# A two-pass attention and MLP kernel on one core: A's block turn moved to the end of the next slot, and u with all that follows one slot later

## The chip, the cores and the metric

The kernel runs on one core of one Trainium2 chip. Its time is the device time of one execution in microseconds; the number to predict is the median of the runs.

## The reference

There are 64 batches, each with x and ctx of 128 x 512 (float32). Every batch goes through the same two layers:

```python
# layer 0, one batch: x_c = x, x_s = ctx (C = 128 rows, T = 512 columns)
Mn = Wn @ inorm(x_c) + bn;  Mm = Wm @ inorm(x_s) + bm
A  = softmax(Mn.T @ Mm, axis=-1)              # 512 x 512
Mo = (Wl @ x_s + bl) @ A.T
x  = Wo @ Mo + bo + x_c
# layer 1: x attends to ctx with 16 heads of 32, then an MLP 512 -> 2048 -> 512
q = LN1(x) @ q_w + q_b;  k = ctx @ k_w + k_b;  v = ctx @ v_w + v_b
hidden = softmax(q k.T / sqrt(32), masked) v @ cproj_w + cproj_b + x
out = hidden + gelu(LN2(hidden) @ fc_w + fc_b) @ proj_w + proj_b
```

## The kernel before

Two passes follow each other. `attention_pass` computes `hidden` for all batches and stores it; `mlp_pass` reads it back in 16 groups of four batches. The change touches only the first pass.

The first pass is a software pipeline written out by hand. Slot `s` handles several batches at once: `b0` is batch s, `b1` batch s-1, up to `b5`, batch s-5 (six in flight); `ahead` is batch s+1. Every engine has its own `slot(s)` with a fixed order of instructions, and engines meet only at semaphores. The slots -1 to 5 are written out, then come loop turns of four slots, then the last ones up to `LAST` = B + 4 = 68. The sum of what one slot does in steady state, in TensorE's order:

- the scores S1 of b4 (mask matmuls and `qT` x `kT`, L1055 and L1060), V of b2, the turn of the normalised x1 of b2 (L999), the two small projections M of b0, one half of the key or query projection of a pair of batches (`qk(0)`; keys in even slots, queries in odd ones), the scores S0 of b0, the product of probabilities and V of b5 (L1101), u = ctx x A.T of b1 (twelve matmuls of 512 columns from `at_hi`, `at_lo`, `ctxT_hi`, `ctxT_lo`), `qk(1)`, layer 0's output (`out0`, which needs `u_hi` and `u_lo`) of b1, and the output projection (`cproj`) of b5.

Each large matmul is made of three passes over an upper and a lower half of each operand (fp32r); the upper half is made by ScalarE, the lower one by VectorE (DVE) or GpSimd (POOL).

A, the softmax of b0, has to be turned (transposed) before it can be used. ScalarE writes the exponentials (L728) and scales them (L747) into `A`; SP writes `A` to `a_turn` in memory in two halves (`write_a`, L497) and reads it back in blocks into `a_blocks` in the next slot (`read_a`, L504, which first waits until that batch's data is in memory and until `at_lo` of the batch before has been computed). DVE then turns 32 x 32 blocks in place (`turn_a`, L844, four instructions), ScalarE makes `at_hi` (`upper_at`, L712), POOL `at_lo` (`lower_at`, L599). The probabilities of layer 1 take the same way through `p_turn` and `p_blocks` (`turn_probs`, L820). All transfers are issued by SP, in the order of its `slot`. DVE's slot has `turn_a(0)` and `turn_a(1)` right behind the lower half of M (L869), `turn_probs` after them, then `turn_a(2)`, `turn_a(3)`, and only then the four `maximum0` (L837) on which the softmax of b0 waits. `ctx` is turned at the end of b0's own slot (L928).

## Time and profile before

| | |
|---|---|
| median of 3 runs | 3541.45 us (3538.01 to 3541.54) |
| the profiled execution | 3546.0 us, span of its instructions 3543.8 us |
| first pass, about | 0 to 2133 us |
| second pass, about | 2133 to 3544 us |
| TensorE busy | 3001.6 us (85%) |
| DVE busy | 1894.7 us (53%) |
| ScalarE busy | 1494.3 us (42%) |
| POOL busy | 1102.1 us (31%) |

The busy times are sums over both passes. TensorE's clock has two levels; the column PEclk gives the share of the higher one that was granted.

### The profile page before, as it was taken

How to read it: one execution, taken by the hardware profiler on the slowest of the kernel's cores; microseconds unless marked ns; L12 is line 12 of the kernel's file. 1: busy time of each engine (PE TensorE's matmuls, PEld its weight loads, DVE VectorE, ACT ScalarE, POOL GpSimd, SP SyncE). 2: the span in 40 equal slices, each digit the busy share in tenths (PEclk: the TensorE clock that was granted, in tenths of full speed). 3: DMA queues.
4: the chain of work that ended last, by engine and by line, in shares of the span. 5: the costliest groups of instructions: out<-in, count | busy, mean ns of one | idle time of the engine just before them, and what ended most of it. 6: DMA issues, size and time to landing. Idle time of an engine off the chain costs nothing. (4 is left out here: it accounts for less than half of the span.)

```text
span 3543.8 us, 54659 instructions
## 1 busy us (share of the span) xinstructions
PE 3001.6 (85%) x17527; PEld 2458.7 (69%) x17527; DVE 1894.7 (53%) x3705; ACT 1494.3 (42%) x4210; POOL 1102.1 (31%) x998
## 2 busy tenths in 40 slices
PE   6777787778777777787778759999999999999999
PEld 4666666656566666666666647888888888888887
DVE  5666666666666666666666645333333333333332
ACT  4665556556655665566556633111111111111111
POOL 4554445444444544444444422000000000000000
PEclk8988898898889888998989878999999999999999
DMA  6555665566566655666566552111111111111110
GB/s 174 162 165 163 176 179 163 163 175 176 160 167 181 173 165 165 181 177 164 168 178 179 161 159 94 39 38 37 36 36 36 36 36 36 36 36 36 36 41 18
DMA packets 440819, 416.04 MB, mean 117 GB/s; under 512 B 155200, under 2 KB 319552, under 8 KB 440768
## 3 DMA queue, kind: packets, MB, share of 16 engines
q1 hardware_dynamic: 440768, 415.40, 42.5%
q8 instruction: 27, 0.44, 0.1%
q14 instruction: 24, 0.20, 0.0%
HBM read 231.79 MB, written 167.77 MB: 113 GB/s over the span
## 5 line engine op out<-in xcount | busy, mean ns | idle before, releaser
L1308 ACT ACTIVATE gl<-pre,fc_bias 128x512 f32<-128x512 f32 x256 | 176.6, 690 | 1119.2 <-PE pre L1393 1119.2
L1347 DVE CAST hT_hi<-gl 128x512 fp32r<-128x512 f32 x256 | 109.3, 427 | 839.8 <-ACT gl L1308 839.8
L599 POOL TENSOR_TENSOR at_lo<-a_blocks,at_hi 128x512 fp32r<-128x512 f32 x256 | 323.0, 1273 | 507.2 <-ACT at_hi L712 499.9
L1101 PE MATMUL bank<-y,stage 128*32 128x128 f32 x2048 | 123.0, 419 | 405.3 <-DVE y L820 405.3
L675 ACT ACTIVATE rows<-bank,negmax 128x128 f32<-128x128 f32 x1024 | 359.2, 365 | 125.1 <-DVE negmax L831 125.1
L1101 PEld LDWEIGHTS bank<-y,stage 128*32 128x32 f32 x2048 | 88.8, 167 | 436.7 <-DVE y L820 375.5
L844 DVE STREAM_TRANSPOSE a_blocks<-a_blocks 128x512 f32<-128x512 f32 x256 | 164.0, 680 | 391.1 <-DMA a_blocks<-a_turn 391.1
L712 ACT ACTIVATE at_hi<-a_blocks 128x512 fp32r<-128x512 f32 x256 | 156.3, 630 | 445.4 <-DVE a_blocks L844 445.4
L590 POOL TENSOR_TENSOR rows<-rows,rsum 128x512 f32<-128x512 f32 x256 | 263.5, 1039 | 225.0 <-DVE rsum L827 225.0
L1392 PE MATMUL pre<-yT_hi,rest_lo 128*128 128x512 f32 x768 | 299.0, 389 | 0.0
L1391 PE MATMUL acc<-rest_lo,hT_hi 128*128 128x512 f32 x768 | 298.9, 389 | 0.0
L1393 PE MATMUL pre<-yT_hi,rest_hi 128*128 128x512 f32 x768 | 298.9, 389 | 0.0
L1393 PE MATMUL acc<-rest_hi,hT_hi 128*128 128x512 f32 x768 | 298.9, 389 | 0.0
L1391 PE MATMUL pre<-yT_lo,rest_hi 128*128 128x512 f32 x768 | 298.9, 389 | 0.0
L1392 PE MATMUL acc<-rest_hi,hT_lo 128*128 128x512 f32 x768 | 298.8, 389 | 0.0
L177 POOL TENSOR_TENSOR rstd<-ve,neghalf 128x4 f32<-128x4 f32 x16 | 16.3, 1018 | 870.9 <-DVE ve L171 870.9
L618 POOL TENSOR_TENSOR normed_lo<-x_ctx,normed_hi 128x512 fp32r<-128x512 f32 x128 | 164.1, 1302 | 309.6 <-ACT normed_hi L752 309.6
L747 ACT ACTIVATE rows<-rows,rsum 128x512 f32<-128x512 f32 x256 | 164.1, 712 | 120.7 <-DVE rsum L920 120.7
L675 ACT ACTIVATION_READ_ACCUMULATOR rows<-bank,negmax 128x1 f32 x1024 | 210.9, 206 | 0.0
L831 DVE TENSOR_REDUCE negmax<-bank 128x4 f32<-128x512 f32 x256 | 169.1, 683 | 44.9 <-PE bank L1060 44.9
L1268 POOL TENSOR_TENSOR rows<-rows,proj_bias 128x512 f32<-128x512 f32 x64 | 83.0, 1299 | 326.2 <-DVE y L183 321.2
L1349 DVE TENSOR_TENSOR hT_lo<-gl,hT_hi 128x512 fp32r<-128x512 f32 x256 | 177.3, 693 | 8.8
(158 smaller groups left out, 8189.2 us busy)
## 6 DMA issues: line engine op xcount, KB each, us to landing
a_turn<-rows SPq DMA_DIRECT2D x128, 512.0 KB, 7.6
a_blocks<-a_turn SPq DMA_DIRECT2D x256, 256.0 KB, 5.1
p_turn<-rows SPq DMA_DIRECT2D x128, 512.0 KB, 3.0
p_blocks<-p_turn SPq DMA_DIRECT2D x256, 256.0 KB, 5.9
x_ctx<-in_x SPq DMA_DIRECT2D x64, 256.0 KB, 2.6
x_ctx<-in_ctx SPq DMA_DIRECT2D x64, 256.0 KB, 2.8
blocks<-in_ctx SPq DMA_DIRECT2D x256, 64.0 KB, 5.7
small<-in_x SPq DMA_DIRECT2D x64, 256.0 KB, 6.0
```

Of the source, the lines that this page charges most:

```text
L590: pool.tensor_tensor(probs[:, :, r, :, :], probs[:, :, r, :, :], rsum1[:, r, :].unsqueeze(1).unsqueeze(3).to_broadcast([P, 4, 4, 32]), ALU ...
L599: pool.tensor_tensor(by_rows(at_lo, j), a_chunks[:, j], by_rows(at_hi, j).bitcast(F32), ALU.subtract).then_inc(at_lo_set, 1)
L618: pool.tensor_tensor(normed_lo[:, i, :], normed[:, i, :], normed_hi[:, i, :].bitcast(F32), ALU.subtract).then_inc(normed_lo_set, 1)
L675: act.activation(probs[:, :, r, c, :], by_chunk(S1_BANK[r])[:, c, :].rearrange("p (d b) -> p d b", b=32), ACT.Exp, bias=negmax1[:, r, c:c ...
L747: act.activation(A[:, :, t, :], A[:, :, t, :], ACT.Identity, scale=rsum0[:, t:t + 1]).then_inc(a_scaled, 1)
L831: dve.tensor_reduce(negmax1[:, r, :], by_chunk(S1_BANK[r]), AX_X, ALU.max, negate=True).then_inc(max1_set, 1)
L1101: mm = pe.matmul(bank[PV_BANK][32 * r:32 * r + 32, c * P:(c + 1) * P], v_sb[:, b5.quarter, h * HD:(h + 1) * HD], pT[:, r, c, :], start=Tru ...
L1308: act.activation(gl[:, i % 2, :], pre[i % 2][:], ACT.Gelu_apprx_tanh, bias=mlp.fc_bias[:, i:i + 1]).then_inc(gelu_done, 1)
L1349: dve.tensor_tensor(hT_lo[:, i % 2, :], gl[:, i % 2, :], hT_hi[:, i % 2, :].bitcast(F32), ALU.subtract).then_inc(hT_lo_set, 1)
L1391: pe.matmul(out, a_hi, b_lo, start=first, stop=False)
L1392: pe.matmul(out, a_lo, b_hi, start=False, stop=False)
L1393: return pe.matmul(out, a_hi, b_hi, start=False, stop=last)
```

## The change

`LOOPED` and `LAST` go from 6 and B + 4 to 7 and B + 5, so the pass has 71 slots instead of 70, and seven batches are in flight. The names are shifted: `a1` is batch s-1, and `b1` to `b5` now mean s-2 to s-6. What belongs to A's turn (`turn_a`, `upper_at`, `lower_at`) and to ctx's turn works on `a1`; u, out0, x1, V, queries, keys, S1 and all behind it work on the shifted names and so come one slot later for a given batch. `turn_a` moves in DVE's slot from before `turn_probs` and `maximum0` to behind `rsum0` and around the normalisation of `ahead`; `upper_at` and `lower_at` move to the end of ScalarE's and POOL's slots. `read_a` stays where it is, at the start of the next slot. TensorE's order of operations is unchanged. No instruction is added to a batch and none is taken away.

```diff
-        FIRST, LOOPED, LAST = -1, 6, B + 4
+        FIRST, LOOPED, LAST = -1, 7, B + 5
@@ sync, slot(s): read_a(s-1) stays first
-                e = s + -1          # x_res
+                e = s + -2
-                e = s + -3          # mask
+                e = s + -4
-                if (s + -4).exists():
-                    write_probs(s + -4, 0)
-                    write_probs(s + -4, 1)
+                if (s + -5).exists():
+                    write_probs(s + -5, 0)
+                    write_probs(s + -5, 1)
...
-                e = s + 1
+                e = s
                 if e.exists() and e.has_before(1):
                     load_blocks(e)
-                e = s + -5          # hidden
+                e = s + -6
@@ gpsimd, slot(s)
-                normalise(0)
-                lower_at(0)
-                normalise(1)
-                lower_at(1)
-                lower_at(2)
-                lower_at(3)
-                normalise(2)
-                normalise(3)
+                for r in range(4):
+                    normalise(r)
                 (in_rstd of ahead)
+                lower_at(0)
+                lower_at(1)
                 (normed_lo of ahead, x1_rstd, x1b, ctxT_lo of a1)
+                lower_at(2)
+                lower_at(3)
@@ scalar, slot(s)
                 exp1(1)
-                upper_at(0)
-                upper_at(1)
                 exp1(2)
                 qk_bias(0)
-                upper_at(2)
-                upper_at(3)
                 exp1(3)
                 exp0(0)
                 exp0(1)
+                exp0(2)
+                exp0(3)
                 (outT_hi of b5)
-                exp0(2)
-                exp0(3)
-                (u_hi of b1)
                 (the four scalings of A)
+                (u_hi of b1)
+                upper_at(0)
+                upper_at(1)
+                qk_bias(1)
+                upper_at(2)
+                upper_at(3)
                 (normed_hi of ahead)
-                qk_bias(1)
                 (ctxT_hi of a1, was b0)
@@ vector, slot(s)
-                turn_a(0)
-                turn_a(1)
                 sum1_reciprocal(1)
                 turn_probs(0..3)
-                turn_a(2)
-                turn_a(3)
-                sum1_reciprocal(2)
                 maximum0(0)
                 maximum0(1)
-                sum1_reciprocal(3)
+                sum1_reciprocal(2)
                 maximum0(2)
                 maximum0(3)
+                sum1_reciprocal(3)
                 (statistics of ahead)
+                (rsum0 of b0)
+                turn_a(0)
+                turn_a(1)
+                (outT_lo of b5)
                 (normed of ahead)
-                (outT_lo of b5)
-                (rsum0 of b0)
+                turn_a(2)
+                turn_a(3)
                 (u_lo of b1)
                 (ctx's turn, x1, mask, x1's statistics, hid: as before)
```

The lines in brackets stand for blocks of the kernel that are moved whole or stay. The first statements of the other engines' slots only change in which parity of s they act.

## Rows read from the trace of the kernel before

**Rows 1.** Stretches of the span: busy (instructions) of PE, PEld, DVE, ACT, POOL; PEclk; DMA share.
```profile
1000.00:1400.00 400.00, 306.73 (x2218) 249.68 (x2217) 264.62 (x524) 241.23 (x745) 190.28 (x174) 0.89 0.62 173
1022.00:1024.00 2.00, 0.00 (x0) 0.00 (x0) 2.00 (x4) 2.00 (x10) 2.00 (x2) 0.50 0.00 0
2300.00:3543.00 1243.00, 1238.60 (x5465) 1025.82 (x5463) 444.45 (x852) 199.15 (x283) 79.79 (x65) 1.00 0.14 35
```
**Rows 2.** The waits, 600 to 1800 us: total us, times, longest.
```profile
PE bank L1101 <- DVE y L820: 236.5, 38, 8.0
DVE a_blocks L844 <- DMA a_blocks<-a_turn: 232.2, 37, 7.8
```
**Rows 3.** DVE's timeline over one slot: start, us, operation, count, [idle before].
```profile
1020.40 1.30 DVE L844 STREAM_TRANSPOSE a_blocks<-a_blocks 128x512 f32<-128x512 f32 x2 [6.99 <-DMA a_blocks<-a_turn]
...
1021.69 2.46 DVE L820 STREAM_TRANSPOSE y<-p_blocks 128x512 f32<-128x512 f32 x4
...
1027.41 0.18 DVE L827 RECIPROCAL rsum<-sum 128x4 f32<-128x4 f32 x1 [0.85 <-ACT rows L675]
...
1031.42 1.00 DVE L909 TENSOR_SCALAR x_ctx<-x_ctx,in_mv,in_rstd 128x512 f32<-128x512 f32 x2 [0.82 <-POOL in_rstd L614]
1032.34 0.68 DVE L807 TENSOR_TENSOR m_lo<-bank,m_hi 128x512 fp32r<-128x512 f32 x1
...
1033.03 0.66 DVE L807 TENSOR_TENSOR m_lo<-bank,m_hi 128x512 fp32r<-128x512 f32 x1
...
1038.92 1.29 DVE L831 TENSOR_REDUCE negmax<-bank 128x4 f32<-128x512 f32 x2 [0.69 <-PE bank L1060]
1040.73 1.43 DVE L853 TENSOR_SCALAR x<-x,x_mv,x_rstd 128x512 f32<-128x512 f32 x1 [0.52 <-POOL stage L630]
...
1044.90 1.38 DVE L869 SCALAR_TENSOR_TENSOR m_lo<-bank,bias,m_hi 128x512 fp32r<-128x512 f32 x2
1053.09 1.30 DVE L844 STREAM_TRANSPOSE a_blocks<-a_blocks 128x512 f32<-128x512 f32 x2 [6.81 <-DMA a_blocks<-a_turn]
```
**Rows 4.** SP's timeline in the same slot: start and us of issuing the transfers.
```profile
1035.97 1.24 SPq L497 DMA_DIRECT2D a_turn<-rows  x2
...
1045.59 1.75 SPq L504 DMA_DIRECT2D a_blocks<-a_turn  x4
```
**Rows 5.** TensorE's timeline in the same slot.
```profile
1024.20 1.93 PE L1101 MATMUL bank<-y,stage 128*32 128x128 f32 x32 [7.13 <-DVE y L820]
...
1033.83 0.47 PE L968 MATMUL bank<-m_lo,small_hi 128*128 128x512 f32 x1 [1.04 <-DVE m_lo L807]
...
1037.57 0.40 PE L1055 MATMUL bank<-mask_less,masked_bf 1*128 1x512 bf16 x4
```
**Rows 6.** GpSimd's timeline in the same slot.
```profile
1036.31 2.56 POOL L618 TENSOR_TENSOR normed_lo<-x_ctx,normed_hi 128x512 fp32r<-128x512 f32 x2 [4.92 <-ACT normed_hi L752]
```
**Rows 7.** ScalarE's timeline in the same slot.
```profile
1033.14 2.56 ACT L747 ACTIVATE rows<-rows,rsum 128x512 f32<-128x512 f32 x4 [2.11 <-DVE rsum L920]
1035.62 1.13 ACT L752 ACTIVATE normed_hi<-x_ctx 128x512 fp32r<-128x512 f32 x2
```
**Rows 8.** The page's groups by cost: A's lower and upper halves, mean ns of one.
```profile
L599 POOL TENSOR_TENSOR at_lo<-a_blocks,at_hi 128x512 fp32r<-128x512 f32 x256 | 323.0, 1273 | 507.2 <-ACT at_hi L712 499.9
...
L712 ACT ACTIVATE at_hi<-a_blocks 128x512 fp32r<-128x512 f32 x256 | 156.3, 630 | 445.4 <-DVE a_blocks L844 445.4
```
**Rows 9.** DVE's timeline at the hid of slots 5, 63, 64 and 68.
```profile
162.36 0.69 DVE L954 TENSOR_TENSOR hid<-bank,stage 128x512 f32<-128x512 f32 x1 [0.74 <-PE bank L970]
...
2032.03 0.69 DVE L954 TENSOR_TENSOR hid<-bank,stage 128x512 f32<-128x512 f32 x1 [0.72 <-PE bank L970]
...
2063.13 0.69 DVE L954 TENSOR_TENSOR hid<-bank,stage 128x512 f32<-128x512 f32 x1 [0.71 <-PE bank L970]
...
2132.91 0.68 DVE L954 TENSOR_TENSOR hid<-bank,stage 128x512 f32<-128x512 f32 x1
```
**Rows 10.** The waits, 0 to 145 us.
```profile
DVE a_blocks L844 <- DMA a_blocks<-a_turn: 10.2, 3, 6.9
```

More of the change, by code:

```diff
@@ L533, in slot @@
                     load(e)
-                if (s + -4).exists():
-                    read_probs(s + -4)
+                if (s + -5).exists():
+                    read_probs(s + -5)
                 if s.exists():
@@ L564, in load_second_for_mlp @@
                 sp.dma_start(mlp_raw[1], mlp_stage_source(w, 1)).then_inc(mlp.staged[1], 16)
-            slots(sp, slot, {B + 1: load_for_mlp, B + 3: load_second_for_mlp})
+            slots(sp, slot, {B + 1: load_for_mlp, B + 4: load_second_for_mlp})
         @block.gpsimd
@@ L584, in slot @@
             def slot(s):
-                b0, b1, b2, b3, b4, ahead = s, s + -1, s + -2, s + -3, s + -4, s + 1
+                b0, a1, b1, b3, b4, ahead = s, s + -1, s + -2, s + -4, s + -5, s + 1
                 def normalise(r):
@@ L666, in slot @@
             def slot(s):
-                b0, b1, b2, b3, b4, b5, ahead = s, s + -1, s + -2, s + -3, s + -4, s + -5, s + 1
+                b0, a1, b1, b2, b3, b4, b5, ahead = s, s + -1, s + -2, s + -3, s + -4, s + -5, s + -6, s + 1
                 def exp1(r):
@@ L680, in qk_bias @@
                 def qk_bias(half):
-                    if s.parity == 0 and b1.exists() and b2.exists():
+                    if s.parity == 1 and b1.exists() and b2.exists():
                         act.wait_ge(k_done, b2.pair_nth(2, half + 1))
@@ L901, in slot @@
                     dve.tensor_scalar(in_ve[:], in_mv[:, :, 1], EPS, None, ALU.add).then_inc(in_veps, 1)
+                if b0.exists():
+                    dve.wait_ge(exp0_done, b0.nth(4, 4))
+                    if a1.exists():
+                        dve.wait_ge(a_scaled, a1.nth(4, 4))
+                    dve.reciprocal(rsum0[:], sum0[:]).then_inc(rsum0_set, 1)
+                turn_a(0)
+                turn_a(1)
+                if b5.exists():
+                    dve.wait_ge(outT_hi_set, b5.nth(1, 1))
+                    lower(outT_lo, bank[PV_BANK][:], outT_hi, outT_lo_set)
                 if ahead.exists():
@@ L910, in slot @@
                                           in_rstd[:, i:i + 1], ALU.subtract, ALU.mult).then_inc(normed_set, 1)
-                if b5.exists():
-                    dve.wait_ge(outT_hi_set, b5.nth(1, 1))
-                    lower(outT_lo, bank[PV_BANK][:], outT_hi, outT_lo_set)
-                if b5.exists() and not b4.exists():
-                    first_group()
-                if b0.exists():
-                    dve.wait_ge(exp0_done, b0.nth(4, 4))
-                    if b1.exists():
-                        dve.wait_ge(a_scaled, b1.nth(4, 4))
-                    dve.reciprocal(rsum0[:], sum0[:]).then_inc(rsum0_set, 1)
+                turn_a(2)
+                turn_a(3)
                 if b1.exists():
@@ L923, in slot @@
                     lower(u_lo, bank[U_BANK][:], u_hi, u_lo_set)
-                if b0.exists():
-                    dve.wait_ge(blocks_in, b0.nth(64, 64))
+                if b5.exists() and not b4.exists():
+                    first_group()
+                if a1.exists():
+                    dve.wait_ge(blocks_in, a1.nth(64, 64))
                     if b1.exists():
@@ L960, in statistics @@
                     mlp.lower_half(dve, mlp.first_lo[:, 0, c, :], mlp.first_hi[:, 0, c, :], 0, c, mlp_raw[0])
-            slots(dve, slot, {0: prepare_small, 2: prepare_q, LAST - 2: statistics})
+            slots(dve, slot, {0: prepare_small, 3: prepare_q, LAST - 2: statistics})
         @block.tensor
```

56 lines of the change are left out of this document (28 added, 28 removed).

## The prediction, made before the changed kernel ran

> **What bounds the kernel now.** I read the stretches first. In the second pass TensorE works all the time at the full clock; in the first pass every engine has gaps (TensorE 307 of 400 us, DVE 265, POOL 190) [rows 1]. So the second pass stays as it is, and the question is what paces a slot of the first. From slot 5 to slot 63 the hid of one batch follows the last after (2032.03 - 162.36) / 58 = 32.24 us [rows 9].
>
> The waits name two large ones of equal size: TensorE stands 236.5 / 38 = 6.2 us a slot until DVE has turned the probabilities, and DVE stands 232.2 / 37 = 6.3 us a slot for the blocks of A to come back from memory [rows 2]. They are one wait: DVE's order puts turn_a ahead of turn_probs and maximum0, so what waits for either waits for A's round trip [rows 3].
>
> The timelines close the circle. A's blocks of one slot are turned from 1020.40, those of the next from 1053.09: 32.69 us [rows 3]. In between: 15.57 us from the turn over maximum0, exp0, rsum0 and the scaling to the issue of the write at 1035.97, then 9.62 us until the write has landed and the read is issued at 1045.59, then 7.50 us until it has landed [rows 4]. The sum is 32.69, with no slack anywhere. This loop of work and two landings is the bound; TensorE's 7.13 us before L1101 [rows 5] are its consequence.
>
> **The change part by part.**
>
> *turn_a behind rsum0.* The round trip no longer stands before maximum0 of the same slot. DVE's wait of 6.99 us goes, if the blocks have landed by the new place. I time a new slot from its mask matmul (0; 1037.57 before). DVE reaches the end of L869 at 8.7, as before (1046.28) [rows 3]. Everything between 1020.40 and u_lo at 1033.03 is the same set of DVE operations in a new order, 12.63 us, of which two waits should go: 0.85 for ScalarE (the exponentials are no longer interleaved with upper_at) and 0.82 for in_rstd (two turns and outT_lo now stand in between) [rows 3]. That leaves 10.96. turn_a(0) comes behind this set without its four turns, outT_lo and the normalisation (about 4.0 us): at 8.7 + 7.0 = 15.7.
>
> *Loop 1, work.* maxima1 to the end of L869: 7.36 (1038.92 to 1046.28); the set: 10.96; start of u_lo to out0: 0.80 (1033.03 to 1033.83); out0 and cproj to the next mask matmul: 3.74; from there to maxima1: 1.35 [rows 3, 5]. Sum 24.21 us a slot. This is DVE nearly without a pause, closed by TensorE.
>
> *Loop 2, landings.* turn_a(0) to the end of the normalisation of ahead: two turns 1.29, outT_lo and a reciprocal 0.69, two normalisations 0.92 = 2.9; then load, read_probs and the issue of write_a, which SP holds in this order behind the normalisation: 3.63 (1032.34 to 1035.97); the two landings 9.62 and 7.50 [rows 3, 4]. Sum 23.65. At 24.2 a slot the blocks have landed 0.6 us before turn_a(0) wants them.
>
> *Loop 3, POOL.* lower_at(0) and (1) now stand ahead of normed_lo, and upper_at ahead of normed_hi. From x1n (1040.73) to the end of L869 5.55, to rsum0 7.0, four scalings 2.5, u_hi with four upper_at and qk_bias 3.5 (0.6 each, 0.8), normed_hi to POOL 0.7, and 4.42 from normed_lo to the next x1n (1036.31 to 1040.73) [rows 3, 6 to 8]. Sum 23.7. POOL's own two lower_at, 2.5 us, run beside ScalarE's part.
>
> *lower_at(2), (3) at POOL's end.* read_a of the next slot waits for them, and x_res, mask and write_probs are queued behind it on SP. POOL ends ctxT_lo about 4 us into the next slot and these at 6.5; the write of A lands at about 7.4 (issue at 22 of a 24.2 us slot, plus 9.62), so they cost nothing while they are under that; uncovered they would cost their excess.
>
> *TensorE.* 32.71 - 7.13 - 1.04 = 24.5 us without its two waits [rows 5], less what half clock costs L1101 and u now: after its pause the granted clock is 0.50 [rows 1]. With no pause over 1.1 us left I expect it to stay at 2.4 GHz, which takes TensorE to about 23 us. If the clock stayed low there, TensorE would be at 24.5 and set the same slot as loop 1, so either answer is inside the range.
>
> *The DVE and POOL overlap.* x1n takes 1.43 us where two of the same form take 1.00, the ones beside no POOL work [rows 3]. It overlaps POOL's work now and will again, so it stays at 1.43. The Trainium skill (SBUF — State Buffer, Who interferes with whom) says that such a DVE instruction and GpSimd hold a common port in turn, and the later one fully blocks. It speaks against the change, which moves more POOL work to that place: by it mask and normalisation could lose up to 0.9 us each. The normalisation falls where POOL has nothing yet; mask lies beside the cproj wait.
>
> *The slot.* Three loops and TensorE lie within 1.2 us of each other, 24.2 the longest. A tie of four is seldom met exactly, so I take 24.8 (0.6 is my allowance, an estimate; the ends are 24.0, all waits at their best, and 27.4, below).
>
> *Fill and drain.* There are 71 slots for 70, one more to fill and one more to drain. Fill: the first hid moves from slot 5 to slot 6, 162.36 + 32.24; against that slots 5 and 6 take 24.8 instead of 32.24, 2 x 7.4, and of the 10.2 us waited for A's blocks before 145 us [rows 10] I count 8 as gone. First hid at about 171.8. Then 57 slots of 24.8 to slot 63: 1413.6, at 1585.4. Slot 64 (no b0; before 31.1 [rows 9]) I put at 24 and slot 65 at 21, both estimates from loop 1 without maximum0 and M; the last four stay 2132.91 - 2063.13 = 69.8 [rows 9]. Last hid at 1700.2 instead of 2132.91: 432.7 us saved.
>
> The profiled execution took 3546.0 us, 4.5 more than the median of 3541.45. 3546.0 - 432.7 = 3113.3, and 4.5 less gives 3109 for the median. One microsecond of the slot is worth some 58 us.
>
> **The rivals.**
>
> *A. The landings grow (loop 2 sets).* For: the same bytes in fewer microseconds bring the DMA share from 0.62 [rows 1] to 0.62 x 32.24 / 24.8 = 0.81, and loop 2 is only 0.6 us below loop 1. Against: what is issued ahead of each of the two transfers, and in which order, stays the same, and between 1022 and 1024 the DMA engines do nothing [rows 1]. It decides once the two landings take over 0.6 us more. At 20% more (3.4 us on 17.1) the slot is 27.1 and the time 3109 + 2.3 x 58 = 3242; at 30%, in the proportion of the share, 28.8 and 3341. The Trainium skill (DMA: Bandwidth & Descriptors, Latency and other measured facts) gives memory access 0.2 us on average and 2 us at high load; by it two landings could rise by 3.6 us, 27.3 a slot and some 3250.
>
> *B. Better than the sum.* Slots at 23.0 to 23.9 us, if x1n and xnT_lo no longer wait (0.52 and more in loop 1) and all halves finish in time: 3109 - 1.3 x 58 = 3034 for 23.5.
>
> *C. The change doesn't take A off the path.* The blocks come later than turn_a(0) by much, since read_a waits for lower_at(3), now POOL's last. The wait then only moves down DVE's slot, in front of normed, u_lo and all that follows. Half of the gain stays: 28.5 to 30, some 3350.
>
> *D. Slower than before.* The same place, the landings on SP's one queue behind POOL's tail. Loop 2 has 17.12 us of landings; it becomes slower than before only when it passes about 32.7 us (the 0.5 above 32.24 for one more drain slot), so when the landings reach 26.2, 1.5 times theirs. At 34 us the time is 3546 + 1.8 x 58 - 4.5 = 3646. Against it: no transfer is added, and the DMA engines have slack.
>
> **How the numbers follow.** Forecast (slots 24.0 to 26.0, 3060 to 3180): 0.62. A: 0.24. B: 0.07. C: 0.04. D: 0.02, and 0.01 for no difference. The predicted time is 3109. The range runs from 3060 to 3255: it leaves out B and D, C and the upper part of A, together 0.2. Faster by over 0.2% (what a measurement of this kernel can tell from no change): 0.97; within it 0.01; slower 0.02.
>
> **What the profile would show.** Right: no wait for a_turn before L844, a slot of some 25 us between two hid, TensorE's wait before L1101 gone and the clock near 1.00 throughout the first pass, L1101 and the twelve matmuls of u at full speed; the largest wait left is TensorE's for u_lo, about 1 us. A would show as a wait of DVE before L844 in its new place, with landings longer than 9.6 and 7.5; C as the same wait of 4 us and more, with read_a issued only after lower_at(3); loop 3 as DVE waiting over 1 us for x1b before L853. The prediction is wrong in its mechanism if the slot stays above 30, and in a size if fill and drain cost more than the 45 us counted for slots 64 and 65.

## The result, and the profile after

| | before | after |
|---|---|---|
| median | 3539.73 us | 3037.14 us |
| runs | 3535.79 to 3541.54 | 3035.83 to 3039.05 |
| span of the profiled execution | 3543.8 us | 3034.5 us |

(The median before is that of the three runs given above and a fourth, 3535.79 us.) The ratio is 0.8582, with a 95% interval of 0.8567 to 0.8597: 502.6 us less. The forecast was 3109 us, the range 3060 to 3255. The direction and the place of the gain came out as forecast; the time is 72 us below the forecast and 23 below the range.

First the stretches of the changed kernel, in the columns of [rows 1] (busy time of PE, PEld, DVE, ACT and POOL, granted clock, DMA share, GB/s). The second pass still does what it did; the first pass has hardly a gap left on TensorE (378.52 of 400 us instead of 306.73), the clock is 1.00 instead of 0.89, and the DMA share has risen from 0.62 to 0.84.

```profile
1000.00:1400.00 400.00, 378.52 (x3004) 314.02 (x3003) 363.19 (x711) 321.01 (x1019) 264.37 (x238) 1.00 0.84 233
1600.00:3034.00 1434.00, 1414.00 (x6239) 1168.42 (x6228) 528.84 (x995) 242.28 (x351) 105.90 (x86) 0.99 0.15 40
```

The waits of the changed kernel between 600 and 1500 us, 38 slots (us in total, times, longest), answer [rows 2]. DVE's wait for A's blocks is 1.4 us in all where it was 6.3 us a slot; TensorE's wait for the turned probabilities is gone; TensorE's largest is now that for u_lo (m_lo, L805, is the helper's name for it), 1.2 us a slot.

```profile
POOL at_lo L599 <- ACT at_hi L710: 112.6, 38, 3.0
...
PE bank L966 <- DVE m_lo L805: 46.9, 38, 1.8
...
DVE x L931 <- PE bank L968: 22.4, 38, 1.0
DVE negmax L829 <- PE bank L1058: 20.9, 38, 0.6
...
DVE a_blocks L842 <- DMA a_blocks<-a_turn: 1.4, 3, 0.6
```

DVE's timeline over one ordinary slot answers [rows 3]: start, us, operation, [idle before and what ended it]. From maxima1 to maxima1 it is 1089.28 - 1065.63 = 23.65 us, and no pause in it is over 0.6 us. (Line numbers are those of the changed kernel, two below the old ones at this place: L829 is maxima1, the row maxima of the scores S1; L842 turn_a; L851 x1n, the normalisation of layer 0's output x1; L867 m_lo; L805 outT_lo, xnT_lo and u_lo. x1n has to wait for x1b, GpSimd's sum of x1 and cproj's bias, which is the tile `stage` at L626.)

```profile
1065.63 1.29 DVE L829 TENSOR_REDUCE negmax<-bank 128x4 f32<-128x512 f32 x2 [0.57 <-PE bank L1058]
1066.87 1.42 DVE L851 TENSOR_SCALAR x<-x,x_mv,x_rstd 128x512 f32<-128x512 f32 x1
...
1071.03 1.38 DVE L867 SCALAR_TENSOR_TENSOR m_lo<-bank,bias,m_hi 128x512 fp32r<-128x512 f32 x2
...
1079.61 1.30 DVE L842 STREAM_TRANSPOSE a_blocks<-a_blocks 128x512 f32<-128x512 f32 x2
...
1082.32 1.29 DVE L842 STREAM_TRANSPOSE a_blocks<-a_blocks 128x512 f32<-128x512 f32 x2
1083.54 0.65 DVE L805 TENSOR_TENSOR m_lo<-bank,m_hi 128x512 fp32r<-128x512 f32 x1
...
1086.79 0.65 DVE L939 TENSOR_SCALAR mask_less<-mask_u 128x128 bf16<-128x128 uint8 x1
...
1089.28 1.29 DVE L829 TENSOR_REDUCE negmax<-bank 128x4 f32<-128x512 f32 x2 [0.57 <-PE bank L1058]
```

TensorE's rows of the same slot answer [rows 5]. The 32 matmuls on the probabilities take 1.08 us instead of 1.93 and start without a wait.

```profile
1076.00 1.08 PE L1099 MATMUL bank<-y,stage 128*32 128x128 f32 x32
1084.33 0.47 PE L966 MATMUL bank<-m_lo,small_hi 128*128 128x512 f32 x1 [1.44 <-DVE m_lo L805]
1087.92 0.40 PE L1053 MATMUL bank<-mask_less,masked_bf 1*128 1x512 bf16 x4
```

SP's rows answer [rows 4]: the write of A is issued at 1062.15, the read at 1071.19, and the turn starts at 1079.61, so from issue to turn there are 17.46 us for the two landings, and nothing else of their slot stands behind them. In the median of 30 slots (batches 20 to 49) the last block has landed 0.7 us before the turn starts. Behind SP's rows stand GpSimd's rows of the piece that matters below (it answers the place of [rows 6]): x1b is done at 1066.77, 0.10 us before x1n starts, and the last lower halves of A end at 1070.70, 6.4 us into the slot, where the prediction had 6.5.

```profile
1062.15 1.22 SPq L497 DMA_DIRECT2D a_turn<-rows  x2
...
1071.19 1.74 SPq L504 DMA_DIRECT2D a_blocks<-a_turn  x4
```
```profile
1065.46 1.31 POOL L626 TENSOR_TENSOR stage<-x,cproj_bias 128x512 f32<-128x512 f32 x1
1066.71 1.30 POOL L629 TENSOR_TENSOR ctxT_lo<-small_t,ctxT_hi 128x512 fp32r<-128x512 f32 x1
1067.96 2.74 POOL L599 TENSOR_TENSOR at_lo<-a_blocks,at_hi 128x512 fp32r<-128x512 f32 x2
```

The hids of slots 6, 63, 64 and 69 of the changed kernel answer [rows 9]. A mean slot is (1511.96 - 163.64) / 57 = 23.65 us; the median of the 57 is 23.57.

```profile
163.64 0.69 DVE L952 TENSOR_TENSOR hid<-bank,stage 128x512 f32<-128x512 f32 x1 [0.20 <-PE bank L968]
...
1511.96 0.69 DVE L952 TENSOR_TENSOR hid<-bank,stage 128x512 f32<-128x512 f32 x1 [0.73 <-PE bank L968]
...
1533.58 0.69 DVE L952 TENSOR_TENSOR hid<-bank,stage 128x512 f32<-128x512 f32 x1 [0.71 <-PE bank L968]
...
1623.57 0.68 DVE L952 TENSOR_TENSOR hid<-bank,stage 128x512 f32<-128x512 f32 x1
```

Last, the page's DMA rows, first of the kernel before and then of the changed one (KB each, median us from issue to landing). With 35% more bytes a microsecond A's two landings are what they were; only the write of the probabilities became longer, 3.0 to 4.5 us.

```profile
a_turn<-rows SPq DMA_DIRECT2D x128, 512.0 KB, 7.6
a_blocks<-a_turn SPq DMA_DIRECT2D x256, 256.0 KB, 5.1
p_turn<-rows SPq DMA_DIRECT2D x128, 512.0 KB, 3.0
```
```profile
a_turn<-rows SPq DMA_DIRECT2D x128, 512.0 KB, 7.6
a_blocks<-a_turn SPq DMA_DIRECT2D x256, 256.0 KB, 5.0
p_turn<-rows SPq DMA_DIRECT2D x128, 512.0 KB, 4.5
```

### The profile page after: what moved, and what is told of

It is laid out like the page before. It is cut to its first block and busy times, and to the rows that moved or that the text cites. A ratio compares the mean times of both kernels' runs of the same rounds, so it can differ in the third digit from the quotient of the medians.

```text
span 3034.5 us, 54536 instructions
## 1 busy us (share of the span) xinstructions
PE 2864.3 (94%) x17527; PEld 2369.3 (78%) x17527; DVE 1910.4 (63%) x3705; ACT 1469.5 (48%) x4210; POOL 1119.3 (37%) x998
## 5 line engine op out<-in xcount | busy, mean ns | idle before, releaser
L599 POOL TENSOR_TENSOR at_lo<-a_blocks,at_hi 128x512 fp32r<-128x512 f32 x256 | 335.4, 1330 | 190.1 <-ACT at_hi L710 190.1
L673 ACT ACTIVATION_READ_ACCUMULATOR rows<-bank,negmax 128x1 f32 x1024 | 239.9, 234 | 0.0
L829 DVE TENSOR_REDUCE negmax<-bank 128x4 f32<-128x512 f32 x256 | 169.0, 682 | 36.7 <-PE bank L1058 36.7
L722 ACT ACTIVATE rows<-bank,negmax 128x512 f32<-128x512 f32 x256 | 178.0, 782 | 10.5 <-DVE negmax L835 10.5
L842 DVE STREAM_TRANSPOSE a_blocks<-a_blocks 128x512 f32<-128x512 f32 x256 | 166.2, 687 | 8.3 <-DMA a_blocks<-a_turn 7.6
L614 POOL TENSOR_TENSOR normed_lo<-x_ctx,normed_hi 128x512 fp32r<-128x512 f32 x128 | 162.2, 1289 | 23.5 <-ACT normed_hi L751 23.4
L835 DVE TENSOR_REDUCE negmax<-bank 128x1 f32<-128x512 f32 x256 | 161.4, 667 | 10.2 <-PE bank L968 10.1
L1389 PEld LDWEIGHTS pre<-yT_lo,rest_hi 128*128 128x128 f32 x768 | 144.3, 188 | 30.0
```

The lines of the kernel that those rows point to most:

```text
L599: pool.tensor_tensor(by_rows(at_lo, j), a_chunks[:, j], by_rows(at_hi, j).bitcast(F32), ALU.subtract).then_inc(at_lo_set, 1)
L673: act.activation(probs[:, :, r, c, :], by_chunk(S1_BANK[r])[:, c, :].rearrange("p (d b) -> p d b", b=32), ACT.Exp, bias=negmax1[:, r, c:c ...
L722: act.activation(A[:, :, t, :], by_chunk(S0_BANK[t]), ACT.Exp, bias=negmax0[:, t:t + 1], accum_out=sum0[:, t:t + 1]).then_inc(exp0_done, 1)
L829: dve.tensor_reduce(negmax1[:, r, :], by_chunk(S1_BANK[r]), AX_X, ALU.max, negate=True).then_inc(max1_set, 1)
L842: dve.transpose(a_chunks[:, j], a_chunks[:, j]).then_inc(at_turned, 1)
L1389: pe.matmul(out, a_hi, b_lo, start=first, stop=False)
```

## The experiments

All ratios are to the kernel before on the same chip. The interval of each is about 0.15% to either side, some 5 us, so two kernels within 8 us of each other aren't told apart by their times; the slots of their traces (one execution each) then help a little further. The two half changes have one run each and no interval. The mean slot is taken over the 57 slots up to slot 63 (58 in the kernels with the old pipeline), the median over the same.

| kernel | median us | ratio, 95% interval | mean slot | median slot |
|---|---|---|---|---|
| before | 3539.73 | | 32.24 | 32.31 |
| changed | 3037.14 | 0.8582, 0.8567 to 0.8597 | 23.65 | 23.57 |
| turns early again | 3546.28, one run | | 31.78 | 31.73 |
| orders alone | 3471.09, one run | | 30.71 | 30.72 |
| A's write first on SP | 3032.31 | 0.8565, 0.8551 to 0.8579 | 23.60 | 23.58 |
| normed halves first | 3029.16 | 0.8546, 0.8531 to 0.8562 | 23.54 | 23.52 |
| u_lo first | 3046.10 | 0.8603, 0.8587 to 0.8618 | 23.79 | 23.59 |
| u_lo and mask first | 3046.61 | 0.8599, 0.8583 to 0.8615 | 23.84 | 23.58 |
| x1n alone | 3031.42 | 0.8565, 0.8547 to 0.8583 | 23.52 | 23.54 |
| one more DVE instruction | 3091.45 | 0.8722, 0.8705 to 0.8739 | 24.57 | 24.08 |
| the same, eight batches a turn | 3108.87 | 0.8774, 0.8751 to 0.8797 | 24.94 | 24.04 |
| all orders together | 3010.84 | 0.8497, 0.8482 to 0.8512 | 23.30 | 23.28 |
| the same, x1n alone | 2980.86 | 0.8420, 0.8402 to 0.8439 | 22.82 | 22.76 |
| the same, u_hi in the middle | 2971.77 | 0.8399, 0.8381 to 0.8417 | 22.63 | 22.62 |

**Which half of the change gives the gain: the later slot, or the order in the slot?** The first kernel undoes the late turns on DVE alone.

```diff
+                turn_a(0)
+                turn_a(1)
                 sum1_reciprocal(1)
                 turn_probs(0)
                 turn_probs(1)
                 turn_probs(2)
                 turn_probs(3)
+                turn_a(2)
+                turn_a(3)
...
                     dve.reciprocal(rsum0[:], sum0[:]).then_inc(rsum0_set, 1)
-                turn_a(0)
-                turn_a(1)
...
-                turn_a(2)
-                turn_a(3)
```

> The changed kernel with one part undone: VectorE's four turns of A's blocks go back to where they stood, two ahead of the turning of the probabilities and two behind it; the later slot of u and of all that follows it, the seven batches in flight and the other engines' orders stay as in the changed kernel. Theory: the gain is that the round of A through DRAM (scaling, write, read, turn) has a whole slot more and no engine stands behind it. With the turns early VectorE again waits for the read of the same round, so the loop of 32.7 us a slot closes again and only the fill differs: a slot of 32 to 33 us and 3530 to 3600 us in all. Rival (the later slot by itself, with its looser ties of u, x1 and the rest, gives the gain): 3050 to 3150 us, with VectorE's wait for a_blocks under 0.5 us a slot.

Measured: 3546.28 us. In its waits (600 to 1500 us) the wait for A's blocks is back, 171.9 / 29 = 5.9 us a slot, and TensorE's for the turned probabilities with it.

```profile
DVE a_blocks L842 <- DMA a_blocks<-a_turn: 171.9, 29, 6.1
PE bank L1099 <- DVE y L818: 171.5, 29, 6.2
```

The later slot of u and of all that follows is worth 0.46 us a slot by itself (32.24 to 31.78), and the longer pipeline pays that back at its ends. The slot is a little under the 32 to 33 us expected, the time is within its 3530 to 3600. The second kernel is the opposite: the old pipeline with the new order on three engines. DVE has its turns, outT_lo and rsum0 where the changed kernel has them; ScalarE's four upper_at stand behind exp0 and the scaling, ahead of normed_hi and u_hi; GpSimd's four lower_at stand behind in_rstd, ahead of normed_lo. It isn't the changed kernel's order to the letter: there u_hi stands ahead of upper_at, which it can't here, since u needs the halves of this very slot.

```diff
-                turn_a(0)
-                turn_a(1)
...
                     dve.reciprocal(rsum0[:], sum0[:]).then_inc(rsum0_set, 1)
+                turn_a(0)
+                turn_a(1)
...
+                turn_a(2)
+                turn_a(3)
                 if b1.exists():
                     dve.wait_ge(u_hi_set, b1.nth(1, 1))
...
+                for j in range(4):
+                    upper_at(j)
                 if ahead.exists():
                     for i in range(2):
                         act.wait_ge(normed_set, ahead.nth(2, i + 1))
...
+                for j in range(4):
+                    lower_at(j)
                 if ahead.exists():
                     for i in range(2):
                         pool.wait_ge(normed_hi_set, ahead.nth(2, i + 1))
```

> The kernel before with one part of the change alone: turns and halves of A stand late in the slot in the order of the changed kernel on VectorE, ScalarE and GpSimd, but they are still those of the batch before with u, x1 and the rest in the same slots as before and six batches in flight. Theory: the round through DRAM is then hidden, but what was to be gained comes back as the chain turn, halves, u, out0 inside the end of the slot, on which the stages behind wait: 30 to 33 us a slot, 3300 to 3560 us. Rival (the order alone is the gain, the later slot only tidies up): 24 to 25.5 us a slot, 3080 to 3180 us.

Measured: 3471.09 us, 30.71 a slot, both within what the theory gave. Its waits (600 to 1500 us) show where the rest stays: the blocks are there in time, but now the matmuls of u stand and wait 205.1 / 30 = 6.8 us a slot for the lower halves of the same slot, and DVE waits 6.05 us for u_hi behind them.

```profile
PE bank L962 <- POOL at_lo L599: 205.1, 30, 7.0
POOL rows L590 <- DVE rsum L821: 198.7, 116, 3.4
DVE m_lo L801 <- ACT m_hi L746: 181.5, 30, 6.1
```

So of 502.6 us the order alone gives some 70 (one run) and the later slot alone nothing; together they give all of it. One wait had two parties, the landing and the matmuls of u, and moving either away leaves the other.

**What sets the slot of 23.65 us?** Four loops were near it in the sum. First the landings.

```diff
+                if s.exists():
+                    write_a(s, 0)
+                    write_a(s, 1)
                 e = s + 2
                 if e.exists() and e.has_before(2):
                     load(e)
                 if (s + -5).exists():
                     read_probs(s + -5)
-                if s.exists():
-                    write_a(s, 0)
-                    write_a(s, 1)
```

> The changed kernel with SyncE's two writes of A ahead of its load of a later batch and ahead of the read of the probabilities; nothing else differs. Theory (the slot of 23.65 us is set by the loop of VectorE's maxima, m_lo, the turns, u_lo, out0 and the scores, not by landings): no change against the changed kernel's 3037 us, within 6 us. Rival (SyncE's queue and the landings one behind another set the slot; the sum gave them 23.65 us): the write leaves about 2 us earlier a slot, and 57 slots give up to 100 us, so 2930 to 3000 us. A third case: the probabilities' read comes later and turn_probs waits for it, 1 to 2 us a slot, 3090 to 3150 us.

Measured: 3032.31 us, the median slot 23.58 against 23.57. The page's row shows what the edit did to the write: from issue to landing 3.3 us instead of 7.6.

```profile
a_turn<-rows SPq DMA_DIRECT2D x128, 512.0 KB, 3.3
```

The write itself leaves 4.7 us earlier in the slot, but the read only 0.5 (in the median of 30 slots 6.54 instead of 7.01 us behind the hid). SP's own waits (600 to 1500 us) say why: the read now waits 4.9 us a slot for GpSimd's lower halves of the batch before, which are made from a_blocks. In the changed kernel it waited 2.8 us for them and then, in 26 of 38 slots, 0.7 us for the write.

```profile
SPq L432 <- POOL at_lo L599: 185.5, 38, 5.3
```

So the landing of the write doesn't set the slot: it was taken off the path and the time stayed within the 6 us expected. That the landing of the read doesn't either is read from DVE's wait of 1.4 us in 38 slots, since this edit hardly moved it.

Then the work. One needless DVE instruction, ahead of u_lo:

```diff
+                if b2.exists():
+                    dve.bn_stats(more_stats[:], x1[:]).then_inc(more_done, 1)
                 if b1.exists():
                     dve.wait_ge(u_hi_set, b1.nth(1, 1))
```

> The changed kernel with one more VectorE instruction a slot, a needless bn_stats of x1 (0.69 us for this form in the changed kernel's timeline) straight ahead of u_lo, behind all that the scaling, the write and the turn of A wait for. Theory (the order of VectorE's own work, closed by the short wait for the scores, is the loop that sets the slot): each slot grows by 0.6 us and the kernel by 34 to 40 us, to 3071 to 3079 us. Rival (landings, GpSimd or TensorE set the slot and VectorE only just keeps up): up to 0.3 us a slot, 3037 to 3055 us.

Measured: 3091.45 us, 54 us more, where I had expected 34 to 40. It moves DVE on by 0.57 us (1098.52 to 1099.09), and the median slot grew by 0.51:

```profile
1098.52 0.65 DVE L920 BATCH_NORM_STATS2 more_stats<-x 128x6 f32<-128x512 f32 x1
1099.09 0.67 DVE L807 TENSOR_TENSOR m_lo<-bank,m_hi 128x512 fp32r<-128x512 f32 x1
```

That is the theory's part: work added between maxima1 and u_lo lengthens the slot nearly one for one, 57 x 0.51 = 29 us. Of the other 25 us, 2 are in the fill and the rest in 13 slots of 25 to 27.3 us, mostly each fourth one; the last experiment of this section is about them.

Taking work away is the other test. u_lo goes ahead of two turns:

```diff
-                turn_a(2)
-                turn_a(3)
                 if b1.exists():
                     dve.wait_ge(u_hi_set, b1.nth(1, 1))
                     lower(u_lo, bank[U_BANK][:], u_hi, u_lo_set)
+                turn_a(2)
+                turn_a(3)
```

> The changed kernel with VectorE's u_lo ahead of its last two turns of A (two turns of about 0.8 us each leave the path from the maxima to out0). Theory: this loop is the bound and becomes 1.2 to 1.6 us shorter, but the loop over GpSimd, with only some 0.35 us of slack by the trace, takes over, and the later turns push GpSimd's last two lower halves: 0.2 to 1.2 us a slot, 2970 to 3030 us. Rival (TensorE or the landings bound the slot): within 6 us of 3037 us.

Measured: 3046.10 us, median slot 23.59: nothing gained, and 9 us over the changed kernel, outside both the theory's and the rival's range (seven of its slots take 24.4 to 26.0 us). TensorE's timeline of that kernel shows one reason: out0 starts and ends early, and then the scores wait for mask_less, which stands on DVE behind the same two turns.

```profile
1045.91 0.40 PE L1053 MATMUL bank<-mask_less,masked_bf 1*128 1x512 bf16 x4 [0.40 <-DVE mask_less L939]
```

So mask_less went ahead of u_lo as well.

```diff
+                if b3.exists():
+                    dve.wait_ge(mask_loaded[b3.parity], b3.dma())
+                    if b3.has_before(1):
+                        dve.wait_ge(s1_done, (b3 + -1).nth(1, 1))
+                    dve.tensor_scalar(mask_less_1[:], mask_u8[:, b3.parity, :], -1.0, None,
+                                      ALU.add).then_inc(mask_set, 1)
                 if b1.exists():
                     dve.wait_ge(u_hi_set, b1.nth(1, 1))
```

> The kernel with u_lo first (3046 us) with one thing more: the mask's conversion on VectorE (mask_less, 0.97 us) goes ahead of u_lo too, so that the scores of the next slot no longer wait for the turns, ctx's turn, x1 and the statistics that stand ahead of it. Theory: u_lo first gained nothing since the first matmul of the scores then waits for mask_less, on the same engine behind the same turns; with it out of the way VectorE's waits for the scores fall away and the slot comes to 22.9 to 23.3 us, 2995 to 3020 us. Rival (something else, TensorE's 22.6 us of work with its starts or GpSimd, holds the slot at 23.5 us): 3035 to 3050 us.

Measured: 3046.61 us, median slot 23.58. The theory that this was the last thing in the way falls: the rival's "something else" holds 23.58. Its timelines name it. DVE, then GpSimd:

```profile
1001.17 1.42 DVE L851 TENSOR_SCALAR x<-x,x_mv,x_rstd 128x512 f32<-128x512 f32 x1 [0.67 <-POOL stage L626]
...
1013.70 0.18 DVE L900 RECIPROCAL rsum<-sum 128x4 f32<-128x4 f32 x1
...
1024.74 1.42 DVE L851 TENSOR_SCALAR x<-x,x_mv,x_rstd 128x512 f32<-128x512 f32 x1 [0.64 <-POOL stage L626]
```
```profile
1017.55 2.54 POOL L599 TENSOR_TENSOR at_lo<-a_blocks,at_hi 128x512 fp32r<-128x512 f32 x2 [2.98 <-ACT at_hi L710]
1020.36 2.52 POOL L614 TENSOR_TENSOR normed_lo<-x_ctx,normed_hi 128x512 fp32r<-128x512 f32 x2 [0.26 <-ACT normed_hi L751]
1022.84 0.54 POOL L620 TENSOR_TENSOR x_rstd<-x_ve,neghalf 128x1 f32<-128x1 f32 x1
1023.36 1.27 POOL L626 TENSOR_TENSOR stage<-x,cproj_bias 128x512 f32<-128x512 f32 x1
```

This is loop 3 of the prediction, closed: x1n at 1001.17, rsum0 at 1013.70 (12.53 us), ScalarE's four scalings and u_hi and its first at_hi until GpSimd starts at 1017.55 (3.85), GpSimd's two lower halves and a wait of 0.26 until normed_lo (2.81), and from there to the next x1n (4.38): 23.57 us. The prediction had 23.7. In the changed kernel it is as long and has 0.10 us to spare, the time between x1b's end at 1066.77 and x1n's start at 1066.87. So loops 1 and 3 are both there with some 23.6 us, and whoever shortens one alone stands before the other.

The counterpart shortens loop 3 alone: the normed rows' halves first, so that GpSimd need not wait for them in the middle. ScalarE's part of the edit is shown; GpSimd's moves normed_lo ahead of lower_at(0) and (1) in the same way.

```diff
+                if ahead.exists():
+                    for i in range(2):
+                        act.wait_ge(normed_set, ahead.nth(2, i + 1))
+                        act.activation(normed_hi[:, i, :], normed[:, i, :], ACT.Copy).then_inc(normed_hi_set, 1)
                 upper_at(0)
                 upper_at(1)
```

> The changed kernel with the halves of the normed rows ahead of the first halves of A: normed_hi ahead of the first two at_hi on ScalarE, normed_lo ahead of the first two at_lo on GpSimd. Theory (GpSimd's chain has slack in the changed kernel): within 8 us of 3037 us. Rival (the chain at_hi, at_lo, normed_lo, projections, m_lo sets the slot): normed_lo is ready 2.6 us earlier and 0.3 to 1 us a slot is gained, 2980 to 3020 us.

Measured: 3029.16 us, median slot 23.52, 0.05 less. The 8 us are the edge of what the times tell apart. The ratios lie further from each other (0.8546 and 0.8582, 13 us, and their intervals don't meet), so something is gained; the mean slot has 57 x 0.11 = 6 us of it, of which 2 are the one slot of 25.8 us that the changed kernel has.

**x1n and GpSimd.** In the changed kernel x1n (1066.87) starts 0.16 us after GpSimd began ctxT_lo (1066.71) and ends at 1068.29, 0.28 us after ctxT_lo does; in [rows 3] it took 1.43 us too, and two of its form take 0.99 together where GpSimd is idle. One wait more on GpSimd takes ctxT_lo from under it:

```diff
                 if a1.exists():
                     pool.wait_ge(ctxT_hi_set, a1.nth(1, 1))
+                    if b1.exists():
+                        pool.wait_ge(x1n_set, b1.nth(1, 1))
```

> The changed kernel with one wait more: GpSimd does not start ctxT_lo before VectorE's x1n (L851) is done. In the changed kernel x1n starts at 1019.74, 0.39 us after GpSimd began ctxT_lo (1019.35 for 1.29 us), and ends 0.28 us after it; it takes 1.18 us, where the same kind of instruction takes 0.49 (L913, two in 0.98) with GpSimd idle. Theory (x1n is held by GpSimd's running instruction, and it lies on VectorE's loop that sets the slot): x1n takes 0.5 us, each slot loses 0.3 to 0.7 us, 2997 to 3020 us; GpSimd's later halves have the room. Rival 1 (x1n's length is its own): it stays at 1.2 us and the kernel at 3037 to 3060 us. Rival 2 (x1n shrinks, but GpSimd's 0.9 us later lower halves hold the read of A or the u matmuls): x1n 0.5 us and 3037 us or more.

Measured: 3031.42 us. x1n takes 0.55 us instead of 1.42, but the slot is the same 23.54 us, and DVE's timeline shows the wait that took its place, for the matmuls of v:

```profile
1013.41 0.55 DVE L853 TENSOR_SCALAR x<-x,x_mv,x_rstd 128x512 f32<-128x512 f32 x1
1013.88 0.69 DVE L831 TENSOR_REDUCE negmax<-bank 128x4 f32<-128x512 f32 x1
1015.08 0.69 DVE L860 TENSOR_TENSOR stage<-bank,v_bias 128x512 f32<-128x512 f32 x1 [0.52 <-PE bank L970]
```

So x1n's length is GpSimd's doing, shown; and 0.87 us less of it is worth next to nothing as long as v comes no earlier. The time fits none of the three cases expected. My theory's second half (it lies on the loop) was too simple. The matmuls of v follow the same scores on TensorE; DVE gets v 4.30 us after the mask's matmul here (1010.78 to 1015.08), where the changed kernel asks for it at 4.56 (1064.26 to 1068.82). So 0.26 us is all that x1n can give there, and ScalarE's xnT_hi, for which DVE now waits 0.38 us instead of 0.25, takes half of it.

**All together.** The orders of the four kernels above (u_lo and mask first, normed halves first, A's write first):

> All of it at once: u_lo and the mask's conversion first on VectorE, the halves of the normed rows first on ScalarE and GpSimd, the writes of A first on SyncE. Theory: VectorE and TensorE are left with their own work, 21.6 and 22.6 us a slot, and few waits: 22.7 to 23.1 us a slot, 2985 to 3008 us, which would beat the changed kernel. Rival (the parts get in each other's way, as the turn of the last two blocks now ends later and GpSimd's last halves with it): 3030 to 3080 us.

Measured: 3010.84 us, median slot 23.28, a little less than the theory asked (2985 to 3008 us and 22.7 to 23.1). With loop 1 out of the way, loop 3 shows what the normed halves give: 0.30 us off the median slot, and what went is the wait of 0.26 before normed_lo. A's write first is in this kernel too; that none of the 0.30 is its doing is read from that wait and not from a run of its own. The time is 36 us below that of the kernel with u_lo and mask first (0.54 us of its mean slot, since the long slots among them went too), where the two edits added here had given 8 and 5 us singly.

Then the wait that keeps ctxT_lo from x1n, the same edit as above, in this kernel:

> The kernel with all orders together (3010.8 us, 23.28 us a slot) with the same wait: ctxT_lo on GpSimd behind x1n. There x1n starts at 1002.70 and takes 1.43 us, to 0.29 us behind the end of ctxT_lo. Theory: x1n takes 0.5 us and VectorE's loop is up to 0.9 us shorter; TensorE with 22.4 us of work a slot is then the nearest bound: 22.6 to 23.0 us a slot, 2972 to 2995 us. Rival (GpSimd or the chain rsum0, scaling, u_hi, u_lo, out0, scores holds): 3000 to 3025 us.

Measured: 2980.86 us, median slot 22.76, both within the theory's range. x1n takes 0.55 us, and here 0.52 us a slot of its 0.87 are gained, 30 us.

Last, in the kernel just shown, u_hi between ScalarE's second and third scaling:

```diff
-                    for t in range(DC):
+                    for t in (0, 1):
                         act.activation(A[:, :, t, :], A[:, :, t, :], ACT.Identity,
                                        scale=rsum0[:, t:t + 1]).then_inc(a_scaled, 1)
                 if b1.exists():
                     act.wait_ge(u_done, b1.nth(1, 1))
                     act.activation(u_hi, bank[U_BANK][:], ACT.Copy).then_inc(u_hi_set, 1)
+                if b0.exists():
+                    for t in (2, 3):
+                        act.activation(A[:, :, t, :], A[:, :, t, :], ACT.Identity,
+                                       scale=rsum0[:, t:t + 1]).then_inc(a_scaled, 1)
```

> The kernel before it in this list with ScalarE's u_hi between its second and third scaling of A instead of behind the fourth. Theory (u_lo on VectorE waits 0.25 us a slot for u_hi, which stands behind four scalings of 0.64 us): the wait goes and 0.1 to 0.3 us a slot with it, 5 to 17 us less than that kernel. Rival (the later end of the scaling delays the write of A, or u_hi was not on the path): within 5 us of it or slower.

Measured: 2971.77 us, 9 us less, within the 5 to 17 expected; the intervals of the two overlap (their own runs, 2970 to 2976 and 2977 to 2983 us on one chip, don't), the median slot fell from 22.76 to 22.62. TensorE is now at work 393.95 of 400 us:

```profile
1000.00:1400.00 400.00, 393.95 (x3140) 329.72 (x3141) 358.17 (x748) 337.07 (x1069) 271.03 (x248) 1.00 0.90 245
```

That is the best version found: 65 us or 2.2% below the changed kernel, 16% below the kernel before. At 22.3 us of TensorE's work in a slot of 22.6 another order has little left to find in the first pass. The landings are back at the limit as well: in 14 of 40 slots DVE waits for A's blocks again.

```profile
DVE a_blocks L848 <- DMA a_blocks<-a_turn: 6.3, 14, 2.8
```

**The long slots of the kernel with one more instruction.** They came in fours, as the batches in the body of the program's loop do. The body was made eight batches long:

```diff
 class Batch(Item):
-    period = 4
+    period = 8
```

> The kernel with one more VectorE instruction (3091 us) with eight batches in the body of the program's loop instead of four; work, orders and waits are the same. There three of four slots take 24.0 to 24.2 us, 0.5 us over the changed kernel's, and each fourth one 25.6 to 27.3 us, with ScalarE 5.4 to 6.5 us without an instruction where that slot begins. Theory: the fourth slot is the turn of the program's loop, where ScalarE starts its next instruction late, so that with eight batches to a turn only each eighth slot is long: some 6 of 13 long slots are left, 7 times 2.5 us or 17 us less, 3068 to 3080 us. Rival (the long slot comes with the batches, by buffers or quarters used in fours, or from elsewhere in the queues): each fourth slot stays long, 3085 to 3095 us.

Measured: 3108.87 us, 17 us more and not 17 less. The long slots did move with the body: its hids show one slot of 30.6 to 34.8 us in each eight, five in all, and a median of 24.04; seven more take 25.6 to 26.0 us, most of them two slots before or behind a long one. But a turn costs more than twice as much. TensorE's timeline at one of them has it standing 5.38 us at the start of the slot with nothing to wait for ("issue"), and DVE and ScalarE behind it (7.04 and 9.94 us):

```profile
770.21 0.62 PE L1057 MATMUL bank<-mask_less,masked_bf 1*128 1x512 bf16 x4 [5.38 <-issue]
```
```profile
773.33 0.37 ACT L675 ACTIVATE rows<-bank,negmax 128x128 f32<-128x128 f32 x1 [9.94 <-DVE negmax L831]
```

Part of the cost comes behind the pause: TensorE's granted clock is 0.50 between 770 and 774 us, and the 32 matmuls of the scores take 1.93 us where they took 1.06 in the changed kernel.

```profile
770.00:774.00 4.00, 3.79 (x40) 3.21 (x41) 1.40 (x3) 0.68 (x4) 0.61 (x1) 0.50 0.48 134
```

The place of the theory holds (the turn of the program's loop), its size doesn't. A lead to the cause stands in the DMA view. Between 600 and 1400 us the queue q8, one of the two that load instructions, moves nothing in the changed kernel and in the one with one more instruction; with eight batches in the body it has 51 packets (number, MB, share of the 16 engines):

```profile
q8 instruction: 51, 0.84, 0.4%
```

Two of its packets and six of the other instruction queue, q14, fall between 766 and 773 us, around TensorE's pause (764.8 to 770.2). This suggests that the longer body is loaded anew in each turn and that TensorE waits for it. No run separates that from other causes, so it stays open.

## Why the prediction was right in its mechanism and 72 us too high

**The bound of before and what the change does to it: right.** The loop of 15.57 + 9.62 + 7.50 us is gone, the wait before turn_a is 1.4 us in 38 slots, TensorE's before the probabilities' matmuls is zero, and what is largest on TensorE is the wait for u_lo with 1.2 us, as the last part of the prediction had it. The two half changes (3546 and 3471 us) show that it is this loop, and that it needs both.

**Loop 1: right in its parts, one of them mis-sized.** The prediction's sum against the slot of 1065.63 to 1089.28:

| | predicted | measured |
|---|---|---|
| maxima1 to the end of m_lo | 7.36 | 6.78 |
| the set, to u_lo | 10.96 | 11.13 |
| u_lo to out0 | 0.80 | 0.79 |
| out0 to the mask's matmul | 3.74 | 3.59 |
| to the next maxima1 | 1.35 | 1.36 |
| sum | 24.21 | 23.65 |

The 0.58 in the first line is DVE's wait of 0.52 us for x1b [rows 3], which I carried over from before. Loop 3's last term already told that GpSimd's x1b would come at its own time and not at DVE's; I should have worked out for the new slot which of the two comes first instead of keeping the old gap. In the changed kernel there is no wait at L851, by the 0.10 us that x1b is ahead of it. The other four lines differ by 0.02 in sum.

**The allowance: the step that failed.** To the longest loop I added 0.6 us for "a tie of four". The slot is the sum of loop 1 and nothing more: 23.65. (Any chain that goes once round the slot has that sum; that this one sets it is shown by its pauses, none over 0.6 us, and by the added instruction, which lengthened the slot by 0.51 us.) The experiments show that a tie was there, of loops 1 and 3 at 23.6, for no single edit moved the median slot by over 0.05 us, and all together moved it by 0.29. But loops that run in parallel don't add to each other, and what would let them meet unluckily, a slot unlike the last, isn't there: all but two of the 57 slots (25.8 and 22.3) lie between 23.4 and 24.3 us. A tie matters for the next change, which will gain nothing from mending one loop, not for this one's time. 57 x 0.6 = 34 us of the error are this, 57 x 0.56 = 32 us the first line of the table.

**Loop 2 and the landings: right that they don't set the slot, and 0.7 us shorter than the sum.** The prediction gave loop 2 23.65 us; here the write's issue to the read's takes 9.04 us (1062.15 to 1071.19) instead of 9.62, and the blocks are there 0.7 us early, so that it is about 22.9. Predicted were 0.6 us to spare, in a slot of 24.2. The landings were the main rival (A). The DMA share came to 0.84, a little above the 0.81 worked out for it, since the slot is shorter, and A's landings stayed at 7.6 and 5.0 us. Rival A would have needed 0.6 us more on the two. The Trainium skill (DMA: Bandwidth & Descriptors, Latency and other measured facts) speaks of an access that grows from 0.2 to 2 us at high load; at a share of 0.90, the most that ran here, the read of A's blocks took 4.9 us and DVE waited 6.3 us for it in 40 slots, all together, so A's rows show no such growth. Rivals C and D needed a loop that never formed.

**TensorE: right.** About 23 us were expected once its clock stayed up; it is 378.52 / 400 x 23.65 = 22.4 us, at a granted clock of 1.00, with the probabilities' matmuls at 1.08 instead of 1.93 us.

**x1n: kept rightly at 1.43, the reason now shown.** It took 1.42 us beside ctxT_lo and 0.55 without it. mask_less behaves alike: mostly 0.65 to 0.76 us in the changed kernel, where normed_lo runs beside it, and 0.22 in the kernels that have it where GpSimd is idle. This is what the Trainium skill (SBUF — State Buffer, Who interferes with whom) says of an instruction that fully blocks, and the trace agrees: x1n ends 0.28 us behind the end of GpSimd's running instruction, though ctxT_lo's successor follows at once. That successor pays in turn: the two lower halves behind it take 2.74 us, and 2.55 in the kernel where x1n is alone. The prediction said that it speaks against the change; it took 0.5 us of mask_less here and not 0.9. That this cost nothing is read from hid behind it, which waits 0.2 to 0.3 us for TensorE anyway.

**Fill and drain.** First hid at 163.64 instead of the 171.8 of the sum: the extra slot of the fill costs 1.3 us net and not 9.4. Slot 64 took 21.6 (24), slot 65 19.7 (21), the last four 70.3 (69.8). Together 11.4 us too high: in all but the last four I was on the careful side.

In all: 8.2 (fill) + 65.5 (57 slots at 1.15) + 3.7 (slots 64 and 65) - 0.5 = 76.9 us, against 1700.2 - 1623.6 = 76.6; the median's error is 4.5 us smaller, since the changed kernel's profiled execution (3036.39 us) lies at its median and not 4.5 above it. The case that came true was rival B, at 3034 us for a slot of 23.5, with half of its reason: x1n no longer waits, but xnT_lo still does, 0.25 us. I gave it 0.07 and left it outside the range. The step at fault is the lower end: I called 24.0 "all waits at their best", but it still held the 0.52 us that B put in doubt, so by the sum's own rows the lower end was 24.2 - 0.5 = 23.7 a slot and some 3045 us, and with the fill's unknown below that. (The upper end of 27.4 a slot stands in none of the prediction's sums, whose nearest are 27.1 and 27.3; it played no part.)

## What to carry to other kernels

A transfer's round trip hides only if both its neighbours move: what it delays before it and what waits behind it; either alone gave nothing and some 70 us here, both 503. When the new loops are summed, the longest was the forecast as it stood here: add nothing for ties where slot is like slot, but work out each carried-over wait anew, for it is a difference of two arrivals and not a cost. After such a change look for loops of equal length and mend them at once; singly the edits here gave 5 to 8 us or a loss of 9, all together 65 (one of the edits, u_hi in the middle, was not tried singly).

## What the runs showed of the hardware

- A VectorE tensor_scalar that starts while GpSimd runs a 1.3 us instruction ends just behind it, x1n by 0.28 us: x1n takes 1.42 us against 0.55, mask_less 0.65 to 0.76 against 0.22. A wait on GpSimd of 0.80 us, which held ctxT_lo back until x1n was done, made the kernel with all orders together 30 us faster, and the changed kernel 6 us, within the noise.
- At a DMA share of 0.84 A's landings took the same 7.6 and 5.0 us as at 0.62; the write of the probabilities went from 3.0 to 4.5 us. What decides the 7.6 us is the place in the queue: with the write issued ahead of the load of x and ctx and of the read of the probabilities it landed in 3.3 us, and in 3.2 at a share of 0.90, while those loads went from 2.6 and 2.9 to 3.2 and 3.6 us. The rows don't say which of the two transfers it had stood behind.
- The turn of the program's loop isn't free. In the changed kernel it is hidden in nearly every slot; once VectorE was the later by 0.5 us it showed as 1 to 3 us in each fourth slot, and with a body of eight batches, where the queue q8 loads instructions throughout, as 7 to 11 us in each eighth.
